# Two mixing stages spread over four engines, and a normalised copy made where it is used

## The reference

```python
x = x + gnn0(layernorm(x))      # three graph layers: mean over neighbours, two products each
x = x + moe0(layernorm(x))      # 8 experts, each row takes its best 2, softmax weights
x = x + gnn1(layernorm(x))      # h = layernorm(x); red = segment_sum(h[src] + rel[type], dst)
                                # GRU: r, z, n from red @ w_ih.T and h @ w_hh.T; (1-z)*n + z*h
x = x + moe1(layernorm(x))      # 16 experts, best 2; y = t + mix; (y-mean)/sqrt(var+eps)*gamma+beta
```

## Time and profile before

| | us |
|---|---|
| median of 3 runs | 1776.88 (1776.11 to 1778.33) |
| profiled execution | 1773.84, its span 1772.1 |
| busy in the span: PE, DVE, ACT, POOL | 1473.6, 871.9, 481.6, 336.9 |
| relate, mixing part | 1040 to 1116 |
| relate, remaining sums | 1116 to 1215 |
| gated unit | 1215 to 1374 |
| combine | 1703 to 1772 |

### The profile page before, as it was taken

How to read it: one execution, slowest core, us unless ns; L and a number is a source line. 1 busy time by engine, 2 the same in 40 slices (tenths; PEclk the granted TensorE clock), 3 DMA queues, 4 the chain that set the end, 5 groups by cost and what they waited for, 6 DMA issues and landing times. The chain is left out here.

```text
span 1772.1 us, 34488 instructions
## 1 busy us (share of the span) xinstructions
PE 1473.6 (83%) x8498; PEld 1031.8 (58%) x8499; DVE 871.9 (49%) x2496; ACT 481.6 (27%) x1231; POOL 336.9 (19%) x391
## 2 busy tenths in 40 slices
PE   4795989989998999975999956998998649999920
PEld 3674744457443855534898932444665638899820
DVE  6996833323222357774222248312888452222258
ACT  2564400012000311112444433001222414444421
POOL 3000210012000300002554420000000514555420
PEclk9555999999999999986999979998999559999965
DMA  4000321123111422222223257202221334332444
GB/s 122 0 0 12 107 75 47 47 75 119 51 50 47 127 91 83 83 76 85 92 95 127 100 155 234 90 24 74 69 67 42 107 134 155 115 115 92 132 129 129
DMA packets 134622, 158.41 MB, mean 89 GB/s; under 512 B 16929, under 2 KB 119698, under 8 KB 134258
## 3 DMA queue, kind: packets, MB, share of 16 engines
q1 hardware_dynamic: 122642, 125.59, 22.4%
q0 software_dynamic: 11840, 32.12, 6.0%
q10 hardware_dynamic: 96, 0.20, 0.0%
HBM read 103.12 MB, written 57.93 MB: 91 GB/s over the span
## 5 line engine op out<-in xcount | busy, mean ns | idle before, releaser
L875 PE MATMUL agg_ps<-parts,counts 128*128 128x512 f16 x1875 | 410.5, 380 | 8.7 <-PEq L653 8.0
L875 PEld LDWEIGHTS agg_ps<-parts,counts 128*128 (+1 forms) x1875 | 183.6, 98 | 227.6 <-issue 13.5
L1441 ACT ACTIVATE experts_hT<-experts_ps_h,experts_b_col 128x128 f32<-128x128 f32 x456 | 165.8, 367 | 186.4 <-PE experts_ps_h L1416 161.1
L1424 PE MATMUL experts_ps_y<-experts_rows,experts_hT 128*128 128x256 f32 x688 | 163.0, 380 | 0.0
L1379 POOL DMA_INDIRECT chosen<-experts_y,experts_row x116 | 114.6, 988 | 146.6 <-issue 107.9
L1368 POOL DMA_INDIRECT experts_fetched<-tokens,experts_index x120 | 116.1, 967 | 93.9 <-ACT experts_x L1445 41.0
L777 POOL TENSOR_TENSOR parts<-proj_rest,gru_rows 128x256 f32 (+2 forms) x75 | 54.4, 726 | 416.8 <-DVE proj_rest L755 416.8
L1424 PEld LDWEIGHTS experts_ps_y<-experts_rows,experts_hT 128*128 128x128 f32 x688 | 124.3, 191 | 13.4
L1416 PE MATMUL experts_ps_h<-experts_xT,experts_rows 128*128 128x128 f32 x976 | 122.1, 279 | 8.9 <-issue 7.8
L1416 PEld LDWEIGHTS experts_ps_h<-experts_xT,experts_rows 128*128 128x128 f32 x976 | 118.9, 194 | 17.5 <-issue 13.8
L1465 DVE COPY experts_xT<-experts_ps_x 128x256 f32<-128x256 f32 x114 | 48.4, 425 | 162.4 <-PE experts_ps_x L1405 162.4
(11 more groups left out here) (314 smaller groups left out, 2039.5 us busy)
## 6 DMA issues: line engine op xcount, KB each, us to landing
experts_rows<-in_L_ffn_w SPq DMA_DIRECT2D x32, 512.0 KB, 4.8
gru_rows<-x SPq DMA_DIRECT2D x75, 128.0 KB, 2.2
own<-proj_own SPq DMA_DIRECT2D x75, 128.0 KB, 1.7
gru_rows<-own SPq DMA_DIRECT2D x75, 128.0 KB, 2.1
h<-agg_out SPq DMA_DIRECT2D x50, 128.0 KB, 1.7
gru_rows<-h SPq DMA_DIRECT2D x50, 128.0 KB, 2.0
gru_rows<-chosen SPq DMA_DIRECT2D x50, 128.0 KB, 2.3
combine_y<-chosen SPq DMA_DIRECT2D x50, 128.0 KB, 2.1
```

The source lines that it names most:

```text
L875: last = nc.tensor.matmul(ps[b][:], cst.counts[:, s, bass.ds(t * P, P)], parts[:, s, :], start=s == 0, stop=s == NT - 1)
L1424: last = nc.tensor.matmul(ps_y[:, 0:D], hT[:, c, :], down[b][:, c, :], start=c == 0, stop=c == KH - 1)
L1441: nc.scalar.activation(hT[:, c, :], ps_h[c][:, 0:P], function, bias=b1_col[:, bass.ds(e * KH + c, 1)]).then_inc(hT_ready, 1)
```

## The change

In both mixing stages ACT multiplies the second choice by its weight, GpSimd adds x (or the tokens) to it, and DVE needs one operation to mix. In relate GpSimd also makes the remainder, and ACT copies each tile's mean into a table; the reciprocals go to a second table. `hn` is no longer stored. The gated unit gets both tables and lets GpSimd make the normalised rows again from x2, with two operations, before TensorE turns them. In combine ACT normalises, with scale and bias, GpSimd multiplies by gamma, and DVE adds the base. DVE finishes tile t-2 in its step for tile t, where it finished t-1 before. The core of the diff:

```diff
 # relate, SyncE: store_normed and its call go
-                    if not early(t - 1):
-                        store_normed(t - 1, b + 1)
 # relate, GpSimd
+                def add(k, b):
+                    pool.wait_ge(scaled, k * B + b + 1)
+                    nc.gpsimd.tensor_tensor(x[b], x[b], y[b][1], ALU.add).then_inc(added, 1)
+                def remain(u, b):
+                    pool.wait_ge(hi_ready, u + 1)
+                    if not early(u - 2):
+                        pool.wait_ge(lo_ready, u - 1)
+                    nc.gpsimd.tensor_tensor(rest[b % 2][:], hn[b % 2][:], tile_of(parts, u)[:, 0:D], ALU.subtract).then_inc(rest_ready, 1)
+                def step(k, b):
+                    t = k * B + b
+                    if not past(t + 1):
+                        add(*behind_by_one(k, b))      # tile t + 1
+                    if not early(t - 1):
+                        remain(t - 1, b + 1)
 # relate, ACT: step is scale(t + 1), split(t - 1), low(t - 2), root(t), and
+                    nc.scalar.activation(y[b][1], y[b][1], ACT.Copy,
+                                         scale=plan.weight[1][:, bass.ds(k * B + b, 1)]).then_inc(scaled, 1)
+                    nc.scalar.copy(mean[:, bass.ds(t, 1)], small[b % 2][:, 6:7]).then_inc(mean_kept, 1)
 # relate, DVE: step is now
+                    dve.wait_ge(added, t + 1)
+                    if not early(t - 2):
+                        dve.wait_ge(stored[d], use * 16)
+                    nc.vector.scalar_tensor_tensor(out[d][:], y[b][0], plan.weight[0][:, bass.ds(t, 1)], x[b],
+                                                   ALU.mult, ALU.add).then_inc(taken, 1)
                     if behind:
                         inverse_of(t - 1, before_d)
+                    if not early(t - 2):
+                        dve.wait_ge(mean_kept, t - 1)
+                    dve.wait_ge(taken, t + 1)
+                    nc.vector.bn_stats(small[d][:, 0:6], out[d][:])
                     if behind:
                         dve.wait_ge(inverted, t)
+                        norm_of(t - 1, before_d)
                     dve.drain()
                     nc.vector.bn_aggr(small[d][:, 6:8], small[d][:, 0:6]).then_inc(var_ready, 1)
 # combine, ACT: step is scale(t + 1), norm_of(t - 1), root(t)
+                def norm_of(u, b):
+                    act.wait_ge(shifted, u + 1)
+                    if not early(u - 2):
+                        act.wait_ge(ready, u - 1)
+                    nc.scalar.activation(normal[b][:], mixed[b][:], ACT.Identity, bias=small[b][:, 10:11],
+                                         scale=small[b][:, 9:10]).then_inc(normed, 1)
 # combine, GpSimd: step is add(t + 1), grade(t - 1)
+                    nc.gpsimd.tensor_tensor(y[b][1][:], y[b][1][:], tile_of(tokens, k * B + b), ALU.add).then_inc(added, 1)
+                    nc.gpsimd.tensor_tensor(normal[b][:], normal[b][:], scale[:], ALU.mult).then_inc(graded, 1)
 # combine, DVE: mix t, reciprocal t - 1, statistics t, then
+                    if behind:
+                        shift_of(t - 1, 1 - d)         # -mean * reciprocal, one column
+                    if not early(t - 2):
+                        last_of(t - 2, use - 1, d)     # waits graded, stored; out = normal + base
 # gated unit, SyncE: one load less
-                    sp.dma_start(x[b][1][:], states[rows(t), :]).then_inc(loaded[b], 16)
-                    sp.dma_start(before[b][:], source[rows(t), :]).then_inc(loaded[b], 16)
+                    sp.dma_start(before[b][:], source[rows(t), :]).then_inc(before_loaded[b], 16)
 # gated unit, GpSimd; TensorE's turn and DVE's product wait for state_ready
+                    pool.wait_ge(before_loaded[b], k * 16 + 16)
+                    if not at_start(k):
+                        pool.wait_ge(used, t - (B - 1))
+                    spread = lambda a: a[:, bass.ds(t, 1)].to_broadcast([P, D])
+                    nc.gpsimd.tensor_tensor(x[b][1][:], before[b][:], spread(state_mean), ALU.subtract).then_inc(state_centred, 1)
+                    pool.wait_ge(state_centred, t + 1)
+                    nc.gpsimd.tensor_tensor(x[b][1][:], x[b][1][:], spread(state_inv), ALU.mult).then_inc(state_ready, 1)
```

More of the change, by code:

```diff
@@ L1565, in _ @@
                 nc.gpsimd.memset(parts[REL_ROW:P, NT - 1, :], 0.0).then_inc(cleared, 1)
+                pool.drain()
+                def add(k, b):
[12 more added lines that the diff above has]
+                        remain(t - 1, b + 1)
+                add(0, 0)
+                loop(pool, step)
+                remain(NT - 1, NT - 1)
             @block.tensor
@@ new lines, in _, with add, grade, step @@
+            def _(pool):
+                def add(k, b):
+                    pool.wait_ge(scaled, k * B + b + 1)
+                    nc.gpsimd.tensor_tensor(y[b][1][:], y[b][1][:], tile_of(tokens, k * B + b), ALU.add).then_inc(added, 1)
+                def grade(u, b):
+                    pool.wait_ge(normed, u + 1)
+                    nc.gpsimd.tensor_tensor(normal[b][:], normal[b][:], scale[:], ALU.mult).then_inc(graded, 1)
+                def step(k, b):
+                    t = k * B + b
+                    if not past(t + 1):
+                        add(*behind_by_one(k, b))
+                    if not early(t - 1):
+                        grade(t - 1, (b + 1) % 2)
+                add(0, 0)
+                pool.wait_ge(w_loaded, 16)
+                loop(pool, step)
+                grade(NT - 1, (NT - 1) % 2)
@@ L1824, in load_gru_rows, with gru @@
         sp.dma_start(w_rows[:, i], ins[n].rearrange("(g p) d -> p g d", p=P)).then_inc(cst.gru_rows_loaded, 16)
-def gru(nc, ins, cst, dr, w_rows, sums, states, source, result, stats):
+def gru(nc, ins, cst, dr, w_rows, sums, source, state_mean, state_inv, result, stats):
     G = 3 * D
@@ L1899, in _, with turn @@
                     pe.wait_ge(done, GC)
-                def turn(b, loads):
-                    pe.wait_ge(loaded[b], loads * 48)
+                def turn(t, b, loads):
+                    pe.wait_ge(loaded[b], loads * 16)
+                    pe.wait_ge(state_ready, t + 1)
                     for i in range(2):
@@ L1923, in step @@
                     last.then_inc(product, 1)
-                turn(0, 1)
+                turn(0, 0, 1)
                 loop(pe, step)
@@ L1997, in _, with step @@
                 finish(NT - 1, (NT - 1) % 2)
+            @block.gpsimd
+            def _(pool):
+                def step(k, b):
+                    t = k * B + b
+                    pool.wait_ge(before_loaded[b], k * 16 + 16)
[5 more added lines that the diff above has]
+                    nc.gpsimd.tensor_tensor(x[b][1][:], x[b][1][:], spread(state_inv), ALU.mult).then_inc(state_ready, 1)
+                loop(pool, step)
 def four_blocks(nc, ins, out):
```

121 lines of the change are left out of this document (54 added, 67 removed).

## The result

The changed kernel takes **1789.11 us** (median of 4 runs, 1787.88 to 1790.11) against 1777.61 for before (4 runs): ratio **1.0060, 95% interval 1.0049 to 1.0072**. It is 0.6% slower, 11.5 us; I had forecast 1771.5 and a range of 1761 to 1784. Run once more on chip 9, with before beside it, it gave 1.0056 (1.0037 to 1.0074).

What follows compares the result with a forecast made beforehand. No engine was full in relate (SyncE's transfers and store waits); DVE was nearly the bound in the gated unit, alone in combine. -6.0 + 5.2 - 4.6 = -5.4 gave a 1771.5 us median; own range 1767 to 1776, overall 1761 to 1784.

Steps and rivals of the forecast that it cites:

- Combine, "-4.6": Last mixing stage: 2.2 us a tile, its end at 1762.3 against 1766.94, so 4.6 us saved.
- the forecast sum: Whole kernel: relate -6.0, gated unit +5.2, combine -4.6, together -5.4 us.
- Two limits lie above it: Combine: loads (1.97 us a tile) and holding (1.74 to 2.26) exceed DVE's own operations, 1.61.
- holding: Combine: two GpSimd operations and two DVE operations that can't run beside them, 1.74 to 2.26 us a tile, taken as 2.2.
- the loads' limit: Combine: SyncE waits for a tile's final result before loading the fifth tile on; 1.97 us a tile.
- the start doesn't move: Relate: the third result waits 2.99 us for a store either way, so the start adds nothing.
- The step of 2.35 a tile: Relate: a loop through the x2 store gives 2.28 us a tile, taken as 2.35, against 2.63 before.
- The term: Relate: 6.3 us saved over 22 tiles, last remainder 0.3 longer on GpSimd: -6.0 us.
- Gated unit, "+5.2": Gated unit: start +1.5 us, DVE's product held 0.4 a tile by GpSimd, +3.7 over 24 tiles.
- the second rival: All three stages: everything is held to GpSimd's end; +1.4 us, 1778.3, no change to be seen; chance 0.22.
- The slower rival: Gated unit: both GpSimd operations meet a DVE one, DVE becomes the bound; at 0.9 held +9.8 us, 1786.7; chance 0.18.

Runs made afterwards that it cites:

- e3: Changed kernel with the last mixing stage (combine) of before; ratio 1.0038 to before, combine 70.9 us.
- c1: Kernel before with only the changed combine; ratio 1.0027 to before, combine 73.2 us.
- n1: Changed kernel with four buffers in place of two for combine's mixed rows; ratio 1.0043 to before, combine 70.6 us.
- n2: Changed kernel without GpSimd's product with gamma in combine; ratio 1.0021 to before, combine 67.9 us.
- k1: Kernel before without store and load of normalised rows; relate keeps tables, ACT remakes the rows in the gated unit; mixing stays on DVE; ratio 0.9982.
- k2: k1 plus relate's split over ACT, GpSimd and DVE, the memset on DVE without GpSimd's drain; ratio 0.9982 to before.
- e6: Kernel before with relate's split alone, normalised rows stored and loaded as before, memset on DVE without GpSimd's drain; ratio 1.0027 to before.
- a1: Changed kernel, unchanged, run again on chip 9; ratio 1.0056 to before.
- e2: Changed kernel with the gated unit of before: relate stores the normalised rows, the gated unit loads them, GpSimd idle there; ratio 1.0068 to before.

## Why the prediction was wrong

- **Combine, "-4.6": the step that failed.** It measured +5.7 to +6.0, a miss of 10.3 to 10.6 us, some 60% of the whole (the forecast sum was -5.4, the pair on chip 9 has +12.0). The exchanges (e3, c1) show 3.6 to 4.3 of the loss as the split's; the rest of it stays open. "Two limits lie above it", loads and holding, left out a third: the loop over two buffers through ACT. It also took holding as a share of the time (2.2 a tile), where it is a meeting that the chain itself arranges: one ACT instruction releases both the gamma product and the mixing. Four buffers (n1) take the loop away and give 4 us back; taking the product away (n2) gives 7. And the loads' limit, worked out as 1.97, was not reached: with the loop or the product gone a tile takes 2.36 or 2.30, and ACT waits for loads in most tiles. Counted as operations that can't run beside GpSimd's were two of DVE; the shift, held as well, was put at 0.08. ACT's normalising took 0.60, for which I had 0.45.
- **Relate, "the start doesn't move":** the first result moved by 6.7 us against the stage's first load, and the third, which the sentence was about, by 4.4 (10.7 to 15.1). The sum has no term for the drain that the diff puts behind the memset. The step of 2.35 a tile was nearly right (2.39 by the same measure), and so was DVE waiting for the x2 store (15 times). What gives the step are both parts together: the store's going half of it (k1), the split the other half (k2), and the split alone nothing (e6). The term was -6.0; it measured -4.0 in the first pair and -1.1 on chip 9, where 2.1 of the difference lie in the part behind the last result.
- **Gated unit, "+5.2":** measured +5.3 on chip 9 and +6.3 in the first pair, a tile 5.82 for 5.78 forecast, the product held by 0.41 for the 0.4 that I took. Right in mechanism and size, though with some luck in the size: the product held was the next one (with the previous state), and it was held in 15 tiles and not in all. The rule that I weighed there (the Trainium skill, SBUF — State Buffer, Who interferes with whom) holds in these rows for operations with two SBUF operands: each product and each mixing that starts while a GpSimd operation runs ends 0.27 to 0.29 after it. The that I called in agreement didn't bear on it: their operation has one such operand. So single operations behaved as in the second rival, whose sum missed in combine all the same.
- **The sum and the rivals:** none was what happened. The slower rival had the right sign for the wrong stage. All rivals varied one question, how much GpSimd holds; drain and buffer loop lay outside of it, so the range (to 1784) was too narrow. The slower rival's 1786.7 comes near the result by chance: its gated unit was to take 6.24 a tile, and took 5.82.
- **The profile pair** overstated the loss by 4.2 us in the experts' stage: its 239.6 is what chip 13 shows, its 243.8 what chips 0 and 9 show. The ratio on chip 9 (1.0056) doesn't contain it.

## What to carry to other kernels

Before spreading work over engines, find what ends the wait in that stage: taking a fifth of DVE's work away left relate's 2.70 a tile as it was (e6), and taking one store off the queue brought 2.57 (k1). Once the store is gone, DVE's work counts: 2.45 (k2). Every buffer that a new engine reads late becomes a loop: count its length with its real operations before you count busy time, and see which two of them are released by the same instruction. A kernel's added drains and their place belong in the sum like any instruction.

## What the runs showed of the hardware

- GpSimd stood idle for 9.34 us at a drain behind a 0.52 us memset, which began 3 us after the start of its last indirect DMA, in after, a1 and e2 alike. What it waits for isn't shown.
- The shift, one column wide, took 0.14 alone and on average 0.33 in combine, up to 0.69: a tiny DVE operation is held like a large one, and ends 0.01 to 0.02 after GpSimd's.
- The holding goes both ways: GpSimd's add, 0.72 in most tiles, took 0.96 to 1.02 where it started beside the shift and the final sum on DVE, which then kept their 0.14 and 0.42 (after, from 1739.66, 1744.75 and 1752.28).
- The second experts' stage, the same code in all kernels, took 4 to 5 us longer on two chips than on a third.
- ACT took 0.60 for 128x256 with a column of scales and one of shifts, 0.505 with a column of scales; a copy of this size took 0.405.
